# A graph network on one core: selections and additions in narrower pieces, open marks on ScalarE, and a count made in an earlier stage

## The reference

```python
# relational part
W = einsum('rb,bio->rio', w_comp, weight)
msg = einsum('ni,rio->rno', relu(layernorm(x)), W)[etypes, src]
x = x + segment_sum(msg, dst, N) + h_bias
# two layers
deg = segment_sum(ones, dst, N); inv_deg = 1 / maximum(deg, 1)
h = leaky(relu(layernorm(x)) @ enc_w + enc_b)            # leaky: slope 0.1
for l in range(2):
    agg = segment_sum(h[src], dst, N) * inv_deg
    h = leaky(agg @ lin_l_w[l] + lin_l_b[l] + h @ lin_r_w[l])
return x + h
```

## Time and profile before

| | |
|---|---|
| median of 3 runs | 3403.03 us (3397.12 to 3404.61) |
| profiled execution | 3396.55 us, span 3394.8 us |
| mean granted TensorE clock | 0.905 of full speed |
| busy: PE, PEld, DVE, ACT, POOL | 2463, 1823, 2901, 1885, 2461 us |
| share of the span: PE, PEld, DVE, ACT, POOL | 73, 54, 85, 56, 72% |
| DMA | 969 MB, mean 285 GB/s |

### The profile page before, as it was taken

One profiled execution on the slowest core, in us unless ns is written; L12 is line 12 of the kernel. 1 busy time (PEld: TensorE's weight loads), 2 busy tenths in 40 slices (PEclk: granted clock), 3 DMA queues, 4 the chain that ended last, 5 costly groups with the idle time before them and its releaser, 6 DMA issues. The chain is left out here.

```text
span 3394.8 us, 49738 instructions
## 1 busy us (share of the span) xinstructions
PE 2463.2 (73%) x13942; PEld 1823.4 (54%) x13942; DVE 2900.7 (85%) x8116; ACT 1885.4 (56%) x4895; POOL 2461.0 (72%) x2412
## 2 busy tenths in 40 slices
PE   2999999999999588888888888657777746663000
PEld 2555555555555366666666666557777735553000
DVE  4899888888888599999999999689999978776567
ACT  1566666666666498888888888635555521110000
POOL 4477777777777477777777777577777757778871
PEclk9999999999999799999999999979999978776555
DMA  9989888887222599999999999479999989999999
GB/s 244 371 325 283 260 235 257 239 258 227 77 82 73 185 282 283 286 284 283 287 284 283 285 285 282 125 254 340 341 333 346 312 314 416 416 416 404 399 407 357
DMA packets 642447, 969.06 MB, mean 285 GB/s; under 512 B 70661, under 2 KB 412295, under 8 KB 630370
## 3 DMA queue, kind: packets, MB, share of 16 engines
q1 hardware_dynamic: 532598, 717.70, 62.9%
q0 software_dynamic: 85376, 194.22, 17.8%
q10 hardware_dynamic: 24198, 53.96, 4.7%
HBM read 509.25 MB, written 464.73 MB: 287 GB/s over the span
## 5 line engine op out<-in xcount | busy, mean ns | idle before, releaser
L972 PE MATMUL y_ps_rel<-w_basis,ht_rel 128*128 128x512 f32 x1568 | 754.3, 605 | 4.0 <-DVE two_rel L831 4.0
L709 POOL DMA_INDIRECT agg<-rows_rel,put_c x392 | 408.0, 1041 | 160.9 <-issue 96.1
L1251 ACT ACTIVATE h_node<-base_node,shift_node,rstd_node 128x128 f32<-128x128 f32 x1176 | 500.3, 483 | 1.6 <-DVE shift_node L1331 1.6
L368 POOL DMA_INDIRECT gat_rel<-in_x_dram,src_c x392 | 406.8, 1038 | 125.1 <-issue 109.9
L1111 POOL DMA_INDIRECT base_and_means<-rows_node,odd_c x392 | 388.1, 990 | 145.9 <-issue 118.0
L1102 POOL DMA_INDIRECT term_node<-agg,src_c x392 | 394.1, 1005 | 132.7 <-issue 119.6
L1792 POOL DMA_INDIRECT gat_l<-base_and_means,src_c x392 | 393.5, 1004 | 119.7 <-issue 119.4
L831 DVE SCALAR_TENSOR_TENSOR two_rel<-y_ps_rel,coef,two_rel 128x128 f32<-128x128 f32 x1568 | 438.4, 343 | 0.0
L972 PEld LDWEIGHTS y_ps_rel<-w_basis,ht_rel 128*128 128x128 f32 x1568 | 273.9, 195 | 199.2 <-issue 138.0
L984 PEld LDWEIGHTS sum_ps_rel<-same_rel,two_rel 128*128 128x128 f32 x1568 | 238.5, 192 | 191.0 <-issue 188.2
L912 ACT ACTIVATE part_rel<-y_ps_rel,coef 128x128 f32<-128x128 f32 x784 | 242.4, 361 | 159.2 <-PE y_ps_rel L972 158.7
(11 more groups left out here) (216 smaller groups left out, 6408.7 us busy)
## 6 DMA issues: line engine op xcount, KB each, us to landing
pairs_l<-base_and_means SPq DMA_DIRECT2D x112, 512.0 KB
base_and_means<-zero_row SPq DMA_DIRECT2D x49, 1024.0 KB
means<-zero_row SPq DMA_DIRECT2D x49, 1024.0 KB, 10.9
first_node<-in_x_dram SPq DMA_DIRECT2D x196, 256.0 KB, 4.1
term_node<-agg SPq DMA_DIRECT2D x196, 256.0 KB, 4.6
x<-base_node SPq DMA_DIRECT2D x196, 256.0 KB, 4.6
base_and_means<-done_node SPq DMA_DIRECT2D x196, 256.0 KB, 4.4
out_dram<-last_z_l SPq DMA_DIRECT2D x98, 512.0 KB, 10.2
```

What stands on the lines that cost most here:

```text
L368: nc.gpsimd.indirect_dma_start(gat_rel[:, m % X_RING, j, :], None, x, bass.IndirectOffsetOnAxis(ap=src_c[:, m * HALF + j:m * HALF + j + 1] ...
L709: nc.gpsimd.indirect_dma_start(agg, bass.IndirectOffsetOnAxis(ap=put_c[:, t:t + 1], axis=0), rows[:, m % KEPT, j, :], None).then_inc(s_sca ...
L972: nc.tensor.matmul(y_ps[(q + j) % 2][:, c * 512:(c + 1) * 512], ht[:, q, j, :], w_basis[:, 4 * c:4 * c + 4, :], start=True, stop=True).the ...
L1251: last = nc.scalar.activation(h[:, n % 2, j * P:(j + 1) * P], base[:, n % SLOTS, j * P:(j + 1) * P], ACT.Relu, bias=shift[:, b % 2, c:c + ...
```

## The change

- `AHEAD` is 6: the setup gathers two half steps more.
- `select` is made tile by tile with a column of `run_c` as the scalar, seven instructions for one (four in the node stage).
- `find_open` of the relational stage is ACT's: relu(1 - run), in the tile loop at j == 3.
- The addition of the node stage is made in two halves of 256 columns.
- The spare rows of `agg` are zeroed in half step 0 and those of `pair` in half step 10; the first scatter waits only for the former.
- How many half steps each part needs is counted in the relational stage with one part a partition, stored to DRAM, and loaded by SP in layer 1.
- The semaphores of the relational stage are cleared together with those of the node stage.
- Code of layer 1 that is not reached is taken out.

```diff
-    AHEAD = 4
+    AHEAD = 6
...
+        waiting = []
         def clear(held):
-            nc.clear_and_free_semaphores(held)
+            nc.clear_and_free_semaphores(waiting + held)
+            waiting.clear()
             nc.all_engine_barrier()
...
# relational stage, POOL
+                        nc.gpsimd.iota(part_i[:], [[0, 1]], base=0, channel_multiplier=LAST).then_inc(s_border, 1)
...
-                                pool.wait_ge(s_spare, 2 * DMA)
+                                pool.wait_ge(s_spare, DMA)
...
# relational stage, SP
-                            if m == 2:
+                            if m == COUNT_AT - 4:
+                                with nc.allow_non_contiguous_dma(reason="the first destination of each half step"):
+                                    sp.dma_start(firsts[0:COUNT, :], dst_s.rearrange("(m e) -> m e", e=HALF * P)[:, 0]
+                                                 .partition_broadcast(COUNT)).then_inc(s_firsts, DMA)
+                            if m == STORE_AT:
+                                sp.wait_ge(s_above, 4)
+                                with nc.allow_non_contiguous_dma(reason="one count of each part"):
+                                    sp.dma_start(need_d.unsqueeze(1), needed[0:COUNT, :]).then_inc(s_firsts, DMA)
+                            if m == 0:
                                 sp.dma_start(agg[N:N + SPARE, :].rearrange("(p j) f -> p j f", p=P),
...
+                            if m == FILL_STEPS:
                                 sp.dma_start(pair[N:N + SPARE, :].rearrange("(p j) (k f) -> p (j k) f", p=P, f=P),
...
# select, in the relational stage and in layer 1 (in the node stage with X_TILES for HALF)
-                            nc.vector.tensor_tensor(same[:, q, :, :], columns(q),
-                                                    run_c[:, bass.ds(m * HALF, HALF)].unsqueeze(2).to_broadcast([P, HALF, P]),
-                                                    ALU.is_equal).then_inc(s_same, 1)
+                            for j in range(HALF):
+                                t = m * HALF + j
+                                last = nc.vector.tensor_scalar(same[:, q, j, :], run_b[:, q, j * P:(j + 1) * P],
+                                                               run_c[:, t:t + 1], None, ALU.is_equal)
+                            last.then_inc(s_same, 1)
...
# relational stage, DVE
-                            nc.vector.tensor_scalar(open_[:, q, :, :], columns(q), 0.0, None, ALU.is_equal).then_inc(s_open, 1)
...
+                        def count_needed():
+                            dve.wait_ge(s_border, 2)
+                            nc.vector.tensor_scalar(limit[:], part_i[:], float(N - LAST), None, ALU.min).then_inc(s_above, 1)
+                            dve.wait_ge(s_above, 1)
+                            dve.wait_ge(s_firsts, DMA)
+                            nc.vector.tensor_scalar(above[0:COUNT, :], firsts[0:COUNT, 1:HALVES], limit[0:COUNT, :], None,
+                                                    ALU.is_ge).then_inc(s_above, 1)
...
+                            nc.vector.reduce_sum(above_n[0:COUNT, :], above[0:COUNT, :], AX.X).then_inc(s_above, 1)
...
+                            nc.vector.tensor_scalar(needed[0:COUNT, :], above_n[0:COUNT, :], 1.0, None, ALU.add).then_inc(s_above, 1)
...
# relational stage, ACT
+                        def find_open(m, q):
+                            act.wait_ge(s_runb[q], use(m, q))
+                            nc.scalar.activation(open_[:, q, :, :], run_b[:, q, :].rearrange("p (t e) -> p t e", e=P),
+                                                 ACT.Relu, bias=ones[:, 0:1], scale=-1.0).then_inc(s_open, 1)
...
# node stage, DVE
-                            nc.vector.tensor_tensor(base[:, q, :], first[:, q, :], term[:, q, :], ALU.add).then_inc(s_base, 1)
+                            for a in range(2):
+                                part = slice(a * (BLOCK // 2), (a + 1) * (BLOCK // 2))
+                                last = nc.vector.tensor_tensor(base[:, q, part], first[:, q, part], term[:, q, part], ALU.add)
+                            last.then_inc(s_base, 1)
...
# layer 1
-                        count_needed(dve)
...
-                            nc.gpsimd.iota(limit_i[:], pattern=[[LAST, COUNT]], base=0,
-                                           channel_multiplier=0).then_inc(s_limits, 1)
...
+                        sp.dma_start(need[:], need_d.unsqueeze(0)).then_inc(s_need, DMA)
```

## The result

The changed kernel takes 3419.5 us (median of 6 runs, 3413.3 to 3439.0) against 3400.1 for the kernel before on the same chip (6 runs): ratio 1.0063, 95% interval 1.0042 to 1.0083. It is slower, where 3401 us and no measurable change was forecast. The profiled execution's span is 3417.6 us against 3394.8, +22.8.

The account below looks back on a forecast made before the run. DVE was taken to bound the node stage and layer 1's gather phase, Pool the relational stage. Terms: -43.3 - 1.0 + 35.4 - 9.9 + 17.5 = -1.3 us, so 3401 us forecast, range 3354 to 3434.

Parts of the forecast that it names:

- The relational stage and the start: Relational stage: half steps hold at 17.64 us, -52.3; later start, +9.0; together -43.3 us.
- ACT's first open marks: Relational stage's first half step: ACT computes `open` first and waits for the run row, adding 0.7 us.
- Pool's backlog: Relational stage: grows 0.55 us a half step to 28 us at half step 50, under the buffers' 35 us.
- The compare of 128 columns: Narrow selections: 0.067 fixed, 0.065 for columns and 0.06 for the scalar column, 0.19 us each.
- The first rival: Narrow selections: scalar column hides behind the instruction before, a compare takes 0.13 us; 3356 us in all; chance 0.19.
- the third: Node stage and layer 1: no half time at 128 columns, a compare takes 0.26 us; 3454 us; chance 0.08.
- the second: Relational stage: seven compares hold Pool for all 1.4 us and it stays the bound; 3437 us; chance 0.13.
- Together +0.36 a group, +35.4 us: Node stage, 98 groups on DVE: halved additions (0.067, three times) plus selection at 0.76 against 0.60 us.
- +0.33 of selection in each of 53 half steps after the start-up, +17.5 us: Layer 1's gather phase: seven narrow compares lengthen each half step's selection by 0.33 us.
- The start: Layer 1: counting on one partition goes, so Pool's stream comes earlier; -9.9 us, bounds -5 and -16.
- The direction: Whole kernel: terms sum to -1.3 us; chances faster 0.39, same within 0.2% 0.28, slower 0.33.
- the range given: Whole kernel's time: 3354 to 3434 us, taking in the 0.13 us compare and most of the Pool-bound case.

Follow-up runs that it names:

- Experiments 1: Changed kernel with one more Pool instruction in the node stage, an unread iota of 24 words ahead of each group's four scatters: ratio 1.0046, median 3406.1 us.
- 2: Changed kernel with the node stage's addition made whole again (512 columns): ratio 0.9980, median 3385.9 us.
- 3: Changed kernel with the node stage's selection made in one instruction of 512 columns again: ratio 1.0038, median 3407.1 us.
- experiment 4: Changed kernel with layer 1's selection made in one instruction of 896 columns again: ratio 0.9984, median 3388.5 us.
- 9: Changed kernel with the constant 5.0 as scalar, not a column, in the narrow compares of the node stage and layer 1: ratio 0.9942, median 3378.9 us.

## Why the prediction was wrong

**The relational stage and the start: right.** Half steps of 17.64 us to the end, no copy waiting for a scatter, -43.4 against -43.3, and undoing the narrow selection costs 27 us. That the sum fits to 0.1 us is partly luck, since two things within it were off and cancelled: the stage started at 83.7 and not 85.8, and ACT's first open marks cost about 3 us and not 0.7. Pool's backlog grew by 0.37 us a half step and not 0.55. Undoing the early zeroing cost 3.6 us.

**The compare of 128 columns: right.** 0.195 us apart against 0.19, put together from the earlier trace rows; with a constant scalar 0.135. The first rival, a hidden scalar column, and the third, 0.26 us, fall. So does the second: from 200 to 1000 us no Pool transfer takes over 1.07 us, so seven compares hold one off by 0.1 us and not by their 1.4.

**The node stage: the step that failed is "Together +0.36 a group, +35.4 us".** Its own parts measured 0.18 for the selection and 0.23 for the halves, 0.41 together (the halves cost 0.075 each and not 0.067). It took for granted that the other instructions of the group keep their lengths, and they do not. The open compare grew by 0.155 us since it now starts 0.63 us behind a Pool transfer's start, 15.2 us over 98 groups; `square_node` shrank by 0.04, 3.9 us. 0.41 + 0.155 - 0.04 = 0.525, against 10.950 - 10.424 = 0.526. Experiments 1 and 2 freed the compare in two unlike ways and got 13 us back; in 3, 4 and 9, where it stayed at 0.63, it stayed long. I had seen DVE hold Pool and did not ask whether Pool holds DVE.

That Pool's transfer holds the compare is shown by those two experiments and by where the compare starts. The 1372 open compares of the fourteen profiled kernels also show which part of the transfer it is. By their start behind the start of the last Pool transfer:

| start behind the transfer's, us | compares | length, us | start + length |
|---|---|---|---|
| up to 0.53 | 684 | 0.41 to 0.44 | up to 0.94 |
| 0.56 to 0.58 | 7 | 0.62 to 0.63 | 1.19 to 1.20 |
| 0.62 to 0.64 | 651 | 0.56 to 0.58 | 1.19 to 1.20 |
| 0.66 | 8 | 0.53 to 0.54 | 1.19 to 1.20 |
| 0.75, 0.77 | 2 | 0.45, 0.43 | 1.19 to 1.20 |
| 0.91 and more | 20 | 0.41 to 0.47 | |

A compare that is held ends 1.20 us behind the transfer's start wherever it began. With its own 0.42 us that is as if it started at 0.78. So a compare that has not begun by some point between 0.53 and 0.56 waits until 0.78, and one that has begun by then is not held.

**Layer 1: the term "+0.33 of selection in each of 53 half steps after the start-up, +17.5 us" was too small.** The start gave 7.8 against 9.9. The selection cost 0.37 in each of 55 half steps; DVE's busy time shows 21 us. The other 7 of the 27.8 are waits for PE, for which the forecast had no term. They vary by more than that between executions, but the medians of the kernels put them with the narrow selection (experiment 4); what makes PE late is left open.

**The direction** fell with these two: two large terms of opposite sign nearly cancelled in the sum, and 14.2 + 10.3 us of error on them outweigh the -1.3 that was left many times over. The result lies inside the range given, but I took the forecast of no change for likelier than a sum like this allows.

## What to carry to other kernels

- Narrow pieces pay where they free another engine that is the bound (27 us in the relational stage, Pool), and cost their fixed part where the engine that runs them is the bound (DVE: 0.41 us in each of 98 groups and 0.37 in each of 55 half steps, 40 and 20 us, and 50 and 28 with what followed from them). Decide for each stage: undoing them in the node stage and layer 1 was worth 77 us, and the kernel that keeps them in the relational stage only takes 3342.7 us, 1.6% less than before.
- Where one engine is released by the other once a group, their instructions meet at the same place in every group (0.63 us in 94 of 98 here), and a shift of 0.2 us can lengthen an unchanged instruction in all of them. After such a change compare the lengths of the instructions that were not touched.
- The first instruction of a stage on an engine is worth a look of its own: a piece of work that waits for a late load holds up all behind it.

## What the runs showed of the hardware

- VectorE's compare of 512 columns with one tensor input is 0.42 us long where it starts 0.29 to 0.31 us behind the start of a Pool indirect transfer, and 0.57 where it starts 0.63 behind one: so the medians of all fourteen profiled kernels. Held compares end 1.19 to 1.20 us behind the transfer's start, whether they began 0.56 or 0.77 behind it, and those that began up to 0.53 behind it are not held. The waiting goes both ways, as DVE's wide instructions lengthen Pool's transfers. The Trainium skill (SBUF — State Buffer, SBUF: two separate sides) says that the pair of ports shared by the two is held for the whole instruction by the one that started first. That does not fit the compare: a compare that starts 0.31 us behind the start of a transfer of 0.97 us is not held at all. One that starts 0.63 behind, and takes 0.33 from start to next start when free, would have let the next one start 1.30 us behind the transfer's start; it did so at 1.11. The profile's spans on POOL are rough, but the 0.31 lies far inside this one.
- A column as the scalar of a VectorE compare costs 0.06 us an instruction (0.195 against 0.135 at 128 columns).
- The same code of layer 1's gather phase took 526 to 562 us in seven profiled executions, the longer the lower TensorE's granted clock was over it (0.98 at 526 us, 0.95 at 540, 0.92 at 562).
- Small VectorE instructions are lengthened too where they meet a Pool transfer's start: `square_node` is 0.20 us long in the 92 groups of the kernel before in which it starts within 0.01 us of one, and 0.16 in the changed kernel, where it meets none.
